# Two transformer blocks on one core: the recurrence's level operations on half the columns, and its operands read in place

## The reference, cut to what matters

```python
def step(S, inp):
    rt, wt, kt, vt, at, bt = inp
    sa = jnp.einsum('bhij,bhj->bhi', S, at)
    S = S * wt[:, :, None, :] + sa[:, :, :, None] * bt[:, :, None, :] + vt[:, :, :, None] * kt[:, :, None, :]
    yt = jnp.einsum('bhij,bhj->bhi', S, rt)
    return (S, yt)
```

## Time and profile before

| | |
|---|---|
| median of 3 runs | 1333.31 us (1327.91 to 1334.1) |
| profiled execution: its span, the only time that the page gives of it | 1345.1 us |
| TensorE (PE) busy | 1226.9 us, 91% of the span |
| VectorE (DVE) busy | 860.2 us, 64% |
| ScalarE (ACT) busy | 572.0 us, 43% |
| GpSimd (POOL) busy | 253.0 us, 19% |
| recurrence, from its first POOL instruction to the finish phase | about 945 to 1200 us |

### The profile page before, as it was taken

The page is one execution under the profiler, slowest core; times in us unless marked ns, Lnnn a source line. Parts: engine busy times, 40 slices in busy tenths (PEclk is TensorE's granted clock), DMA queues, the critical chain, the costliest instruction groups (busy, mean ns, idle before and its releaser), DMA issues. The chain is left out here.

```text
span 1345.1 us, 32608 instructions
## 1 busy us (share of the span) xinstructions
PE 1226.9 (91%) x13048; PEld 709.8 (53%) x13080; DVE 860.2 (64%) x1737; ACT 572.0 (43%) x857; POOL 253.0 (19%) x433
## 2 busy tenths in 40 slices
PE   6889999999999999889989977996899999979998
PEld 3523333333333333265656644443788888867775
DVE  7487888887888888057222263898566766664432
ACT  3416767777767777732223204563112111112221
POOL 4400010001000100020466500224311222300000
PEclk9959999999999999999999997998899999999999
DMA  4501211111222110060242230000200000000000
GB/s 128 77 2 17 41 29 27 28 27 27 38 39 32 27 29 4 8 218 0 69 143 87 77 123 0 1 1 0 81 4 4 3 4 4 3 3 0 16 16 32
DMA packets 33836, 49.47 MB, mean 37 GB/s; under 512 B 11995, under 2 KB 22331, under 8 KB 32955
## 3 DMA queue, kind: packets, MB, share of 16 engines
q1 hardware_dynamic: 29211, 36.55, 12.1%
q0 software_dynamic: 3744, 10.23, 2.4%
q10 hardware_dynamic: 768, 1.05, 0.2%
HBM read 23.63 MB, written 9.31 MB: 24 GB/s over the span
## 5 line engine op out<-in xcount | busy, mean ns | idle before, releaser
L671 DVE TENSOR_REDUCE at_block_max<-at_p_ring 128x4 f32<-128x512 f32 x576 | 367.8, 686 | 75.1 <-PE at_p_ring L577 42.6
L648 ACT ACTIVATE at_probs<-at_p_score,abias 128x1024 f32<-128x1024 f32 (+2 forms) x320 | 318.9, 1029 | 125.1 <-PE at_p_score L607 70.6
L577 PE MATMUL at_p_ring<-kt,qt 64*128 64x128 bf16 (+3 forms) x1152 | 187.2, 284 | 15.0 <-DVE at_block_max L671 6.9
L622 PE MATMUL at_p_out<-at_probs,at_vs 128*32 128x512 f32 (+3 forms) x1536 | 165.5, 503 | 0.4 <-ACT at_probs L648 0.4
L601 PE MATMUL at_p_score<-qt,kt 64*128 64x512 bf16 (+3 forms) x768 | 146.5, 332 | 5.7 <-ACT at_probs L648 4.8
L577 PEld LDWEIGHTS at_p_ring<-kt,qt 64*128 64x128 bf16 x1152 | 69.9, 95 | 126.9 <-DVE at_block_max L671 86.6
L714 POOL TENSOR_TENSOR at_shift<-shift,at_row_max 128x16 f32<-128x16 f32 x32 | 7.1, 222 | 422.8 <-DVE at_row_max L677 422.8
L601 PEld LDWEIGHTS at_p_score<-qt,kt 64*128 64x128 bf16 x768 | 38.4, 94 | 86.7 <-ACT at_probs L648 54.4
L2098 ACT COPY rc_ta<-rc_bank 128x256 f32<-128x256 f32 x32 | 10.4, 375 | 149.8 <-PE rc_bank L1852 149.8
L2240 PE MATMUL fi_p_in<-fi_xt,w_in 128*128 128x512 f32 x128 | 62.4, 611 | 0.7 <-ACT fi_xt L2276 0.7
L607 PE MATMUL at_p_score<-anticausal,ident 128*128 128x128 bf16 (+1 forms) x384 | 62.9, 246 | 0.0
(11 more groups left out here) (346 smaller groups left out, 2155.8 us busy)
## 6 DMA issues: line engine op xcount, KB each, us to landing
qt<-qparts SPq DMA_DIRECT2D x96, 64.0 KB, 2.5
kt<-kparts SPq DMA_DIRECT2D x96, 64.0 KB, 2.5
rows<-moe_chosen SPq DMA_DIRECT2D x4, 1024.0 KB, 4.8
w_routed<-in_w_routed_dram SPq DMA_DIRECT2D x1, 2816.0 KB
x<-in_x_dram SPq DMA_DIRECT2D x4, 512.0 KB, 8.9
moe_table<-rows SPq DMA_DIRECT2D x4, 512.0 KB, 2.7
out_dram<-x SPq DMA_DIRECT2D x4, 512.0 KB, 2.9
w_down<-in_w_down_dram SPq DMA_DIRECT2D x1, 1408.0 KB
```

The source lines that it names most:

```text
L577: mm = pe.matmul(bank[:, col:col + nb * P], qt[nxt][h * ROWS:(h + 1) * ROWS, pair, t * P:(t + 1) * P], kt[nxt][h * ROWS:(h + 1) * ROWS, pa ...
L622: mm = pe.matmul(p_out[32 * h:32 * h + 32, left(k):QC], vs[(now - e[2]) % BUFS][:, key, h, :], probs[g % PROBS][:, h % 2, at:at + w], star ...
L648: act.activation(probs[g % PROBS][:, :, 0:len(pairs) * w], p_score[g % 2][:, :, 0:len(pairs) * w], ACT.Exp, bias=abias[:, c * TPB + key:c ...
L671: dve.tensor_reduce(dst, src, AX.X, ALU.max).then_inc(s["fill_used"], 1)
```

## The change

VectorE's level operations take only the columns that a level can change: Z and X those with j mod 2m < m, Y the others. Z gets a buffer of its own for each level and batch element, whose other half is cleared once by VectorE at the phase's start. TensorE's products still take all 64 columns. The staging copies, their buffers and their semaphore are dropped, and TensorE reads the time-mixing tensors themselves; at and rt are put into one tensor, so that one product can still read both.

```diff
+JOIN = L // 2
...
-        bt, kt, vt = sb("bt", [P, EH, P]), sb("kt", [P, EH, P]), sb("vt", [P, EH, P])
-        ar = sb("ar", [P, EH, 2 * P])
...
-        X, Y, Z = sb("X", [P, RH, L]), sb("Y", [P, RH, L]), sb("Z", [P, RH, L])
+        X, Y = sb("X", [P, RH, L]), sb("Y", [P, RH, L])
+        Z = {m: sb(f"Z{m}_", [P, RH, L]) for m in INNER}
...
+        def join_columns(t, m, side):
+
+            return t.rearrange("p (n s c) -> p n s c", s=2, c=m)[:, :, side, :]
+
...
                 def turn(t, b):
-                    pe.wait_ge(staged[b], t + 1)
...
-                    for n, (a, c) in enumerate(((bt, kt), (ar, vt))):
+                    for n, (a, c) in enumerate((("bt", "kt"), ("at", "vt"))):
                         for h in range(EH):
-                            pe.transpose(bank[b][:, n, h * P:(h + 1) * P], a[b][:, h, 0:P], ident[:, :])
-                            mm = pe.transpose(bank[b][:, n, (2 + h) * P:(3 + h) * P], c[b][:, h, :], ident[:, :])
+                            pe.transpose(bank[b][:, n, h * P:(h + 1) * P], src(a, t, b)[:, h, :], ident[:, :])
+                            mm = pe.transpose(bank[b][:, n, (2 + h) * P:(3 + h) * P], src(c, t, b)[:, h, :], ident[:, :])
...
-                def both(b, r, half, cols):
-                    return ar[b][r, half, :].rearrange("p (k c) -> p k c", k=2)[:, :, cols]
+                def both(t, b, r, half, cols):
+                    at = t * P + b * S
+                    return data["at_rt"][r, :, half, :, :].rearrange("p k n c -> p k (n c)")[:, :, at + cols.start:at + cols.stop]
...
                 def zy(m):
                     def stage(t, b):
+                        if t == 0:
+                            pe.wait_ge(z_clear[b], INNER.index(m) + 1)
                         pe_wait(pe, t, b, dve=f"z{m}")
...
-                def per_head(b, n):
-                    return bank[b][:, n, 0:RH * L].rearrange("p (h c) -> p h c", h=RH)
+                def joined(b, n, m, side):
+                    return bank[b][:, n, 0:RH * L].rearrange("p (a s c) -> p a s c", s=2, c=m)[:, :, side, :]
+
+                def columns(t, m, side):
+                    return t[:, :, :].rearrange("p h (n s c) -> p (h n) s c", s=2, c=m)[:, :, side, :]
 
                 def z(m):
                     def stage(t, b):
                         need(t, b, f"z{m}")
-                        did(b, dve.tensor_tensor(Z[b][:, :, :], per_head(b, 1),
-                                                 over_heads(level_masks[:, LEVELS.index(m), :]), ALU.mult))
+                        mask = join_columns(level_masks[:, LEVELS.index(m), :], m, 0)
+                        did(b, dve.tensor_tensor(columns(Z[m][b], m, 0).rearrange("p (h n) c -> p h n c", h=RH),
+                                                 joined(b, 1, m, 0).rearrange("p (h n) c -> p h n c", h=RH),
+                                                 mask.unsqueeze(1).to_broadcast([P, RH, JOIN // m, m]), ALU.mult))
...
-                        did(b, dve.tensor_tensor(buf[b][:, :, :], per_head(b, n), buf[b][:, :, :], ALU.add))
+                        side = {"x": 0, "y": 1}[kind]
+                        grown = columns(buf[b], m, side)
+                        did(b, dve.tensor_tensor(grown, joined(b, n, m, side), grown, ALU.add))
...
+                for m in INNER:
+                    for b in range(B):
+                        dve.memset(columns(Z[m][b], m, 1), 0.0).then_inc(z_clear[b], 1)
...
             def _(pool):
-                def stage(t, b):
-
-                    pool.tensor_copy(ar[b][:, :, 0:P], src("at", t, b))
-                    pool.tensor_copy(ar[b][:, :, P:2 * P], src("rt", t, b))
-                    pool.tensor_copy(vt[b][:, :, :], src("vt", t, b))
-                    pool.tensor_copy(kt[b][:, :, :], src("kt", t, b))
-                    pool.tensor_copy(bt[b][:, :, :], src("bt", t, b)).then_inc(staged[b], 1)
-
...
-        data = {n: sb(n, [P, EH, NB, TB]) for n in "rt at bt kt vt gt bonus".split()}
+        data = {n: sb(n, [P, EH, NB, TB]) for n in "bt kt vt gt bonus".split()}
+        data["at_rt"] = sb("at_rt", [P, 2, EH, NB, TB])
+        data["at"], data["rt"] = data["at_rt"][:, 0, :, :, :], data["at_rt"][:, 1, :, :, :]
```

More of the change, by code:

```diff
@@ L1748, in recurrence_phase @@
         state = [sb(f"state{c}_", [P, EH, RN]) for c in range(2)]
-        made, dve_did, act_did, staged = sem("made"), sem("dve_did"), sem("act_did"), sem("staged")
-        y1_made = sem("y1_made")
+        made, dve_did, act_did = sem("made"), sem("dve_did"), sem("act_did")
+        y1_made, z_clear = sem("y1_made"), sem("z_clear")
         hop_made, hop_done, y_out = sem("hop_made"), sem("hop_done"), sem("y_out")
@@ L1827, in stage @@
                                 mm = pe.matmul(bank[b][cols, banks[par], half * width:(half + 1) * width],
-                                               rows_of[b][r, half, cols], rhs(b, r, half, cols),
+                                               src(rows_of, t, b)[r, half, cols], rhs(t, b, r, half, cols),
                                                start=True, stop=True, skip_group_check=True)
@@ L1831, in against_own @@
                     return stage
-                def both(b, r, half, cols):
-                    return ar[b][r, half, :].rearrange("p (k c) -> p k c", k=2)[:, :, cols]
+                def both(t, b, r, half, cols):
+                    at = t * P + b * S
+                    return data["at_rt"][r, :, half, :, :].rearrange("p k n c -> p k (n c)")[:, :, at + cols.start:at + cols.stop]
                 def a1(t, b):
-                    against_own(bt, (2, 3), 2 * L, both)(t, b)
+                    against_own("bt", (2, 3), 2 * L, both)(t, b)
                 def a2(t, b):
                     pe_wait(pe, t, b, act="tok")
-                    against_own(kt, (0, 1), 2 * L, both)(t, b)
+                    against_own("kt", (0, 1), 2 * L, both)(t, b)
                 def a3(t, b):
                     pe_wait(pe, t, b, dve="a1")
-                    against_own(ar, (2, 3), L, lambda b, r, half, cols: bt[b][r, half, cols])(t, b)
+                    against_own("at", (2, 3), L, lambda t, b, r, half, cols: src("bt", t, b)[r, half, cols])(t, b)
                 def per_head(n, lhs, rhs, width=L):
@@ L1864, in stage @@
                         pe_wait(pe, t, b, dve="x1" if m == 2 else f"x{m // 2}")
-                        per_head(1, lambda b, r, h, half, par: ab[b][r, par, half, 0, :],
-                                 lambda b, r, h: X[b][r, h, :])(t, b)
+                        per_head(1, lambda b, r, h, half, par: ab[b][r, par, half, 0, :], lambda b, r, h: X[b][r, h, :])(t, b)
                     return stage
@@ L1873, in stage @@
                         pe_wait(pe, t, b, dve=f"z{m}")
-                        per_head(2, lambda b, r, h, half, par: Y[b][r, h, :], lambda b, r, h: Z[b][r, h, :])(t, b)
+                        per_head(2, lambda b, r, h, half, par: Y[b][r, h, :], lambda b, r, h: Z[m][b][r, h, :])(t, b)
                     return stage
@@ L1878, in stage @@
                     def stage(t, b):
+                        if t == 0:
+                            pe.wait_ge(z_clear[b], INNER.index(m) + 1)
                         pe_wait(pe, t, b, dve=f"z{m}")
-                        per_head(3, lambda b, r, h, half, par: Z[b][r, h, :], lambda b, r, h: Y[b][r, h, :])(t, b)
+                        per_head(3, lambda b, r, h, half, par: Z[m][b][r, h, :], lambda b, r, h: Y[b][r, h, :])(t, b)
                     return stage
@@ L2115, in _ @@
             def _(pool):
-                def stage(t, b):
-                    pool.tensor_copy(ar[b][:, :, 0:P], src("at", t, b))
-                    pool.tensor_copy(ar[b][:, :, P:2 * P], src("rt", t, b))
-                    pool.tensor_copy(vt[b][:, :, :], src("vt", t, b))
-                    pool.tensor_copy(kt[b][:, :, :], src("kt", t, b))
-                    pool.tensor_copy(bt[b][:, :, :], src("bt", t, b)).then_inc(staged[b], 1)
                 for b in range(B):
                     pool.memset(state[0][b][:, :, :], 0.0).then_inc(hop_done[b], 1)
-                    stage(0, b)
                 def y1(t, b):
@@ L2144, in _ @@
                 for t in range(TPB - 1):
-                    for b in range(B):
-                        pool.wait_ge(made[b], t * PE_MARKS["each"] + PE_MARKS["a3"])
-                        stage(t + 1, b)
                     for b in range(B):
```

## The result

The changed kernel takes 1319.95 us (median of 4 runs, 1317.89 to 1323.09) against 1332.19 (1327.91 to 1334.1) for the kernel before, measured beside it: a ratio of 0.9919, 95% interval 0.9895 to 0.9943, or some 11 us less (the medians differ by 12.2; 25 later runs of the kernel before have a median of 1331.08, which makes it 11.1). Forecast were 1324.4 us and a gain of 8.9.

What follows compares the result with a forecast made beforehand. TensorE waiting on single VectorE instructions at six places per round was taken to bound the recurrence; 6.2 + 0.5 + 2.2 = 8.9 us off the 1333.3 us median gives 1324.4 us, range 1317 to 1332.

Steps and rivals of the forecast that it cites:

- six places: Each recurrence round: Z of b=0 (b=1 at level 2) and the last Y, alone on TensorE's path; 0.77 us saved per round.
- Part 2: Rounds 1 to 7, staging dropped: without the copy, X's second addition for b=1 shortens 0.07 us each, 0.5 us; bounds 0 and 0.5.
- Part 3: Recurrence's start: without staging TensorE begins 1.9 + 0.3 = 2.2 us earlier, all on the path; bounds 1.1 and 3.0.
- memsets: Phase's start: ten VectorE memsets, 1.0 to 3.0 us, hide behind turn and a1; bare they would cost 1 to 3 us.
- rival C: turn and a1 to a3: TensorE reads large tensors worse than copies; a quarter more cancels the gain, half gives 1342.7 us; 0.07.
- A: Level operations: larger fixed part, 373 ns throughout, so each place saves 0.05 us; 2.4 plus 2.2, giving 1328.7 us; chance 0.14.
- D: Level waits end on something other than the shortened VectorE instruction; only the start is gained, 1331.1 us; chance 0.10.
- B: Path as forecast, but at the start the clock keeps its instant and the copy is innocent: 7.3 us, 1326.0 us; chance 0.16.
- parts 1: Recurrence levels, half the columns: shorter VectorE instructions save 0.77 us per round, 6.2 us over eight; bounds 4.3 and 6.9.

## Why the prediction was right, and where it was not

The reading was right: at six places TensorE waits for one VectorE instruction and gets back exactly what that one saves, and only Z and the last Y count. Forecast were 6.2 us, measured 6.6 (0.80 us per round where I had 0.77). The difference in the round is level 2, 0.14 us shorter and not 0.095: I gave its runs of two 330 ns, between two rows, and they take no more than 293. The Trainium skill's rule on runs of two ("Vector Engine (DVE) Microarchitecture Reference", Measured stream behaviour on trn2) was the better estimate.

Part 2 failed as to its cause: 0.5 us were counted for a copy that had no part in it. I had excluded POOL's Y additions because the b=0 instruction, which also had one beside it for 0.2 us, was fast. That was no control: the b=1 instruction has one beside it for hardly longer, 0.22, and is slow; beside b=0 VectorE's instruction ran first, beside b=1 POOL's did. Measured gain: nothing, and 0.5 lay in the other instruction, of which the prediction's sentence by the Trainium skill's rule had already kept half back.

Part 3 was too small, 2.2 where 2.8 to 3.0 were measured. The wait for POOL (1.94 us) and the second element's 0.29 were right; the rest, 0.6 to 0.8 us, fits the clock's return, 3.5 us behind the first transpose in place of 5.2 (1.7 us less at half pace are 0.85). The twelve traces without staging have it at 3.3 to 3.8, the one with staging put back at 4.6; why it comes earlier is not shown. The bound of 3.0 held it. The memsets were hidden, and reading the large tensors cost nothing: from turn's first transpose to w0 it is 4.57 us before (1008.58 to 1013.15) and after (988.28 to 992.85), so rival C is out.

Rivals A and D fell with the groups' means of 288 and 291 ns and the rounds; B with the clock, though its other half, that the copy is innocent, came true.

That the sum came so near is partly luck. For 6.2, 0.5 and 2.2 the stretches gave 6.6, 0 and 2.9, so what part 2 counted in excess stands against what parts 1 and 3 left out: 8.9 against 9.47. The median itself is 4.5 us below the 1324.4: 0.6 of these are the stretch, 1.1 the fourth run of the kernel before, which moved its median from 1333.31 to 1332.19, and 2.8 lie in no term of the prediction; the other phases scatter by more (the first mark alone lies between 925.9 and 931.0 in the traces of the changed kernel and its variants).

## What to carry to other kernels

Count a VectorE saving by the places where TensorE waits for exactly that instruction, times the saving of one; here 144 of 224 halved instructions brought a sixth of a steady round's gain (0.14 of 0.80 us). Then look what else the timeline offers at such a place: an addition that nobody needs, queued ahead of the one awaited, was worth 4.5 us, and putting another batch element's stage into the latency 7.0, more than the halving itself. Compare a stretch between two marks of the trace when a change is smaller than the scatter of the other phases.

## What was not expected of the hardware

- Products of 64x64 by 32 columns keep the pace of those by 64: 16 in 0.93 us, 58 ns each, on two quarters of the array.
- With them the granted clock fell to 0.54 to 0.84 over stretches of 20 us, so to 1.2 GHz for part of them, while TensorE had work 93% of the time or more; with the level-16 wait shortened one stretch had 0.91 and the rest 1.00.
- The clock's return behind a pause differs between the traces at the same place, 4 or 12 us behind the second mark in the two shown, by enough to make the finish phase 137.3 or 141.4 us long: some 4 us, a third of this change's effect.
- A VectorE addition with two SBUF inputs takes 495 to 503 ns instead of 424 to 426 when it starts 0.22 us before the end of POOL's two-input addition, and is not longer when POOL's starts 0.2 us before its end; then POOL's is, 790 ns instead of 721 to 729.
